# Attention over top-64 keys: a tile of a wide block and a tile of a narrow block share a step

## The reference

```python
x = x + 0.5 * ffn(layernorm(x));  x = x + attn(layernorm(x));  x = x + 0.5 * ffn(layernorm(x))

def attn(x, ...):                       # x: 4 x 1024 x 256, 16 heads of 64
    q, k, v = x @ Wq, x @ Wk, x @ Wv    # 4 memory keys and values stand ahead of k and v
    dots = einsum('bhid,bhjd->bhij', l2norm(q), l2norm(k)) * 10
    dots = einsum('hg,bgij->bhij', W_pre_th, dots)          # heads mixed
    dots = where(causal, mask_value, dots)
    vk = top_k(dots, 64)[0][..., -1:]                       # the 64th largest of a row
    attn = softmax(where(dots < vk, mask_value, dots))
    attn = einsum('hg,bgij->bhij', W_post_th, attn)         # heads mixed again
    out = einsum('bhij,bhjd->bhid', attn, v) * head_scale
    return (out * sigmoid(x @ Wg + bg)) @ Wo
```

## Time and profile before

| | |
|---|---|
| median of 3 runs | 3987.81 us (3987.8 to 4001.88) |
| the profiled execution | 3988.18 us, of which 3986.4 us span |
| PE busy | 3372.0 us, 85% of the span |
| DVE busy | 2934.9 us, 74% |
| ACT busy | 2528.9 us, 63% |
| POOL busy | 2038.6 us, 51% |
| DMA | 466.45 MB, 117 GB/s on average |
| attention, first to last operation | about 986 to 3709 us |

### The profile page before, as it was taken

How to read it: one execution, slowest core, us unless ns; L and a number is a source line. 1 busy time by engine, 2 the same in 40 slices (tenths; PEclk the granted TensorE clock), 3 DMA queues, 4 the chain that set the end, 5 groups by cost and what they waited for, 6 DMA issues and landing times. The chain is left out here.

```text
span 3986.4 us, 72866 instructions
## 1 busy us (share of the span) xinstructions
PE 3372.0 (85%) x22948; PEld 2142.8 (54%) x22948; DVE 2934.9 (74%) x6615; ACT 2528.9 (63%) x5825; POOL 2038.6 (51%) x5777
## 2 busy tenths in 40 slices
PE   4999999996788988888888857888988888988798
PEld 3444444442455655755555644555566555556566
DVE  3887777777478888667888876788886788887254
ACT  1343333333478789767888936788896788888231
POOL 0021222221577667577766737676675776667232
PEclk8999999999589999969999977899998899999899
DMA  2122222213455565245655314455543555651110
GB/s 105 69 95 84 80 84 86 79 75 115 124 148 164 165 170 134 71 126 159 169 169 167 97 40 129 144 170 169 166 107 82 143 156 167 171 137 51 52 33 27
DMA packets 362422, 466.45 MB, mean 117 GB/s; under 512 B 29524, under 2 KB 294100, under 8 KB 361560
## 3 DMA queue, kind: packets, MB, share of 16 engines
q1 hardware_dynamic: 361944, 461.02, 39.4%
HBM read 226.57 MB, written 234.36 MB: 116 GB/s over the span
## 5 line engine op out<-in xcount | busy, mean ns | idle before, releaser
L1005 ACT ACTIVATE junk<-D,nt 128x76 int8<-128x76 f32 (+62 forms) x1440 | 1070.6, 746 | 176.6 <-POOL nt L1090 138.5
L917 PE MATMUL banks<-kr,E 128*128 128x128 f32 (+1 forms) x4672 | 739.2, 309 | 190.5 <-issue 93.1
L917 PEld LDWEIGHTS banks<-kr,E 128*128 128x128 f32 (+1 forms) x4672 | 631.7, 211 | 302.9 <-issue 280.1
L890 PE MATMUL banks<-Sg,kpre 128*128 128x109 f32 (+51 forms) x1568 | 653.2, 517 | 17.7 <-DVE D L1211 8.7
L876 PE MATMUL banks<-kT,qT 64*128 64x343 f32 (+11 forms) x896 | 408.9, 540 | 182.3 <-DVE Sn L1200 161.1
L1028 ACT ACTIVATE AT<-banks 128x512 f32<-128x512 f32 (+3 forms) x768 | 346.0, 479 | 336.5 <-PE banks L937 169.5
L1290 DVE SCALAR_TENSOR_TENSOR E<-D,vk,E 128x12 f32<-128x12 f32 (+56 forms) x512 | 378.6, 757 | 211.0 <-DVE vk L1246 136.3
L1200 DVE COPY Sn<-banks 128x686 f32<-128x686 f32 (+7 forms) x448 | 376.9, 841 | 138.8 <-PE banks L877 127.1
L1226 DVE SCALAR_TENSOR_TENSOR W<-SG,sgn,W 128x76 f32<-128x76 int8 (+14 forms) x480 | 413.2, 900 | 83.7 <-POOL W L1106 81.7
L554 DVE RECIPROCAL a_ri<-a_rr 128x512 f32<-128x512 f32 x128 | 429.2, 3353 | 4.4
L937 PE MATMUL banks<-AT,V 128*64 128x64 f32 x9216 | 368.6, 232 | 56.4 <-issue 42.0
(11 more groups left out here) (188 smaller groups left out, 5547.0 us busy)
## 6 DMA issues: line engine op xcount, KB each, us to landing
score_scratch<-Sn SPq DMA_DIRECT2D x96, 343.0 KB, 3.2
q_scratch<-a_qn SPq DMA_DIRECT2D x32, 512.0 KB, 2.8
v_scratch<-a_vo SPq DMA_DIRECT2D x32, 512.0 KB, 3.7
k_scratch<-a_qn SPq DMA_DIRECT2D x32, 512.0 KB, 2.7
gate_scratch<-a_gs SPq DMA_DIRECT2D x32, 512.0 KB, 2.7
kT<-k_scratch SPq DMA_DIRECT2D x32, 512.0 KB, 4.8
qT<-q_scratch SPq DMA_DIRECT2D x32, 512.0 KB, 6.3
gateT<-gate_scratch SPq DMA_DIRECT2D x32, 512.0 KB, 11.8
```

The costliest lines, as they stand in the source:

```text
L890: out = nc.tensor.matmul(bank[:, 0:c], kpre[:].rearrange("p h r -> p (h r)"), Sg[:, g % 3, c0:c1], start=True, stop=not diagonal)
L917: out = nc.tensor.matmul(ps[5 + i % 2][0:rows, c % 4 * P:(c % 4 + 1) * P], E[:, g % 4, c * P:c * P + rows], kr[:, g % 4, :], start=True, s ...
L1005: nc.scalar.activation(out, D[:, e, 1:1 + n], ACT.Sign, bias=nt[:, r, e:e + 1], scale=-1.0, accum_out=cnt[:, r, e:e + 1]).then_inc(s[f"cnt ...
```

## The change

**Pairs.** A step no longer takes two tiles that follow each other. `place(g)` gives odd `g` a tile of a narrow block and even `g` a tile of a wide block: block 0 goes with block 7, 1 with 6, 2 with 5, 3 with 4. The wide lane runs 4 steps behind (`LAG`), so there are 260 steps, of which the first four have only a narrow tile and the last four only a wide one. Every other step has about 1040 keys in sum. The steps of batches follow each other without a boundary: the wide lane of pair 4-3 still runs while the narrow lane has begun with block 0 of the next batch.

**Buffers.** `Sg`, `SG`, `junk`, `W` and `E` are split into a wide and a narrow one, `D` has both side by side, `Sg` has two buffers for each lane (four in all), `qT` and `gateT` have two blocks. The wide tile is mixed into banks 2 and 3 (4 too for three pieces), the narrow tile into bank 4. `AT` holds both lanes, from either end.

**Order.** Count 3 and count 1 begin with the narrow tile, and `turned` stands behind count 3 in each step. `sides` and `closest` are two calls each, the wide tile's first, and stand in different slots. `SG` is free after `sides`, `W` after `closest`. `judge` has one operation less. `values` is cut in four quarters: one ahead of the unit in slot 1, one behind it, two at the start of the next step. `select` takes the narrow tile first.

**Units and loads.** Units of both blocks of a pair are made in 12 of 16 steps ahead of it, and a piece has at most 400 columns instead of 512 (in effect block 6 is cut in three pieces instead of two): 480 units instead of 448. The first pair's wide block is scored in the first two steps. Keys of a batch are loaded at once (all eight chunks), over four steps near the end of the batch before, as are values; the means of all blocks are worked out at once (`fore`) and copied when needed (`mean`).

```diff
 def pieces(n):
-    k = -(-n // 512)
+    k = -(-n // 400)
...
+LAG = 4
+NP = B * TURN
+S = NP + LAG
...
+def place(g):
+    w = g // 2 if g % 2 else g // 2 - LAG
+    if not 0 <= w < NP:
+        return None
+    i = w % TURN // TPB
+    return w // TURN, i if g % 2 else IB - 1 - i, w % TPB
...
+    def unit_steps(k):
+        q = (k - 2) // 16 + 1
+        j = (k - 2) % 16
+        slots = [range(0)] * 4
+        if k < 2:
+            n = UC[2] - UC[1]
+            return [range(UC[1] + n * (4 * k + i) // 8, UC[1] + n * (4 * k + i + 1) // 8) for i in range(4)]
...
             for k in range(S + 6):
-                held = (k - 5) % 4 == 0
-                if 0 <= k - 5 < S and not held:
-                    turned(2 * (k - 5))
-                if searched(k - 2):
-                    count(2 * (k - 2), 3)
-                    count(2 * (k - 2) + 1, 3)
...
+                count(k - 2, 3, True)
+                if 0 <= k - 5 < S:
+                    turned(2 * (k - 5))
...
+                count(k - 1, 1, True)
                 if 0 <= k - 5 < S:
                     turned(2 * (k - 5) + 1)
...
+            for i in range(UC[1] - 1):
+                scored([i])
+            for c in range(IB - 1):
+                fore(0, c)
+            scored([UC[1] - 1])
...
+                if k >= 12 and (k - 12) % 4 == 0 and (k - 12) // 4 < NV:
+                    values((k - 12) // 4, 0)
+                units(slots[1])
+                if k >= 12 and (k - 12) % 4 == 0 and (k - 12) // 4 < NV:
+                    values((k - 12) // 4, 1)
+                units(slots[2])
```

818 lines of the change are left out of this document (444 added, 374 removed).

## The result

The changed kernel takes **4154.9 us** (4 runs, 4151.6 to 4159.2) against 3989.3 us before: ratio 1.041 (95% interval 1.0385 to 1.0431), 166 us slower. I had forecast 3914 us, and the range to 4020 doesn't hold it. The profiled execution of the change spans 4157.4 us.

A forecast was written before the change was run, and what follows sets the result against it. DVE's work and flag stall (floor 8.86 us of a 10.3 us step) were taken as the bound, plus waits. Step 3 at 1105, 2482 for 259 steps and 26 for the search put the last exponentials at 3613: 3914 us, range 3825 to 4020.

The forecast's parts named there:

- The start: Run up to step 3: loads, key sums and 24 units of block 7 make it 93 us later than before.
- step 3 at about 1105: Sign for the run's beginning: first exponentials of step 3 at about 1105 us; at 1080 or 1130 it was mis-sized.
- The general search: Its one run, on a flagged row, now meets one wide and one narrow tile: 26 us instead of 40.6.
- at cost nothing: Keys and values loaded by batch over four steps are covered; if values aren't, some 3 us per step, 12 per batch.
- a load by batch holds up SP's queue: Sign named for being wrong: loading keys or values by batch stalls SP's DMA queue; no price given.
- The even step of 9.8 us: 233 uniform steps in the middle take 9.8 us each, 2283 us in all; ends 9.35 and 10.35.
- block 3 is the pattern: Uniform steps resemble block 3 of the kernel before: near the batch's mean load, 78.8 us per eight steps, 9.85 each.
- The end: Last steps, mostly without units: 16 at 8.3 us, four with only a wide tile at 6, two at 5.
- C: Rival, uneven products: TensorE's lumps of values and `post` cost as before; step 10.1, 3984 us, no change; chance 0.18.
- D: Rival, slower: POOL's small search operations, held up by DVE's long rows, lie on the path; step 10.3, 4031 us; chance 0.17.
- D's other sign: In the profile after, waits of PE for `AT` would show that POOL's small operations lie on the path.
- B: Rival, waits shrink: DVE's floor paces, DVE over 86% busy; step 9.35, 3809 us; chance 0.23.

The follow-up runs named there:

- e1: Changed kernel with each values load of 124 rows cut into one of 112 and one of 12 rows: 4044.4 us, ratio 1.0154.
- e2: Kernel before the change with the same cut of its values loads into 112 and 12 rows: 3932.8 us, ratio 0.9876.
- e7: e1 with each values event multiplying only its first chunk, the other chunks' products left out: 3923.7 us, ratio 0.9817.
- e12: e1 with VectorE's select over only the first half of each tile's columns: 3991.7 us, ratio 1.0013.
- e13: e1 with ScalarE's exponentials over only the first half of each tile's columns: 4039.3 us, ratio 1.0122.
- e9: e1 with even values events, five chunks for a wide block and four for a narrow one, same sum: 4039.2 us, ratio 1.0152.
- e4: e1 with ScalarE's count 3 of the wide tile moved behind that lane's `turned`: 4083.1 us, ratio 1.0248.
- e5: e1 with TensorE's `post` of the wide tile moved behind the next step's first mix: 4226.5 us, ratio 1.0595.
- e6: e1 with the second half of each values event behind the first mix, and gating behind the first take: 4063.8 us, ratio 1.0192.
- e11: e1 with the first slot of units behind both mixes and both takes: 4042.0 us, ratio 1.0168.
- e15: e1 with the first wide block's units on alternating banks (4014.0 us), plus unread TensorE products in steps without units or event: 4032.3 us, ratio 1.0125.

## Why the prediction was wrong

**The start: right as a sum.** 1121 forecast for step 5, 1121.7 measured in the change. The sign that I had named for it, step 3 at about 1105, did not come: step 3 begins at 1040.8, and 81 us for two steps stand behind it, since most of the 24 units lie behind step 3 and not ahead of it. The terms held one by one: the key sums take 11.6 us (12), the units 65 (67), and they end at 1094.4 where the sum had 1095.

**The general search: right.** The eight steps with it take 116.5 us where those of another batch take 89.2 (steps 83 to 90, 147 to 154): 27 us, forecast 26, before 40.6.

**The loads of values "at cost nothing": the step that failed first.** I had weighed bytes (2.4 MB per step, 245 GB/s) and priced the case that they aren't covered at "some 3 us per step, 12 per batch". Measured: two such loads per step cost 28 us per batch in their four steps against the cut version, 101 to 111 us in all. The price missed not the bytes but the spread: the loads kept under 4 packets in flight, two loads' packets took 12.5 to 14.6 us, longer than a step, and small loads behind them landed after 13 to 17 us. I had the load in view as a volume, and its form stood in the code, unchanged by the edit. Before, the same load stood alone in a block and cost 1.6 us, hidden among others; four steps with two each made it a queue. My last sentence, "I am wrong [...] if a load by batch holds up SP's queue", named a sign that came: two issues of these loads took 6.9 to 8.1 us together in each batch. I had given it no price of its own, and it is at most a part of the 28 us: the largest waits shown above are for loads and stores that landed late.

**The even step of 9.8 us: the step that failed second.** With the loads mended a step of batch 2 is 10.24 us: 233 steps by 0.44 are 103 us. The stretch itself agrees: steps 7 to 240 of e1 take 2413.6 us, where my sum has 2283 + 26 = 2309, 104 us more. The choice that failed was "block 3 is the pattern". It has VectorE's mean load (64.1 to 64.0 us), but TensorE's is 67.1 against a mean of 71.1, and ScalarE's 62.9 against 65.5. Between blocks 3 and 4, by TensorE's row, 71.1 us of work lie at 78.8 + 4.0/8.6 x 7.5 = 82.3 us, 10.3 a step. The same sum over e2's blocks, which have the loads mended as e1 has, gives 10.1 by TensorE's row (76.5 and 89.1 us at 65.2 and 78.9 us of TensorE, mean 70.2) and 9.8 by VectorE's; 10.24 was measured. These sums were made after the result. I had put TensorE aside by a rule of the Trainium skill (Perfetto Trace Analysis, "Identifying the Most-Contended Engine") that matmul busy time isn't a good measure of how close TensorE is to its roofline. By that row the sum comes within 0.1 us a step, and without it it missed by 0.44; so here the trace doesn't support the rule as I used it, to leave TensorE out of the comparison. (Its loads' row adds up to 388 us, 59% of the batch, and not 393; ScalarE in block 3 is busy 80%, not 81. Neither changes the sum.) What is shown is that TensorE's amount counts (e7, 121 to 134 us of 170), VectorE's in part (e12, 53 to 56 of 134), ScalarE's exponentials hardly (e13), and that neither the evening of large and small events (e9), nor four orders (e4, e5, e6, e11), nor added products at a higher granted clock (e15) brings anything. The steps with an event, which TensorE fills, are a part of it that the trace shows. That the end of the other steps is set now by one engine and now by another, and evening out the tiles doesn't change how often, fits all of this; it is argued and not shown by a run of its own.

**The end: 30 us short.** From step 240 to step 262 the sum has 133 + 24 + 10 = 167 us, and the change took 196.9: 151.4 for the 16 steps at 8.3, 45.5 for the last six, of which I had made 34. In e1 it is 192.5. No run looks into this stretch, so its cause stays open; it is what these steps take without units that was sized too low.

**The sum again**, by the marks of the two profiled executions (the change's took 4159.2 us): 3914 + 1 (start) + 110 (steps 7 to 240, the change against e1: the loads) + 104 (the same steps of e1 against the sum) + 30 (end) = 4159. Nothing of size is left over. Alone, the loads make it 4024 and the longer steps 4018, near the upper end of the range; together they leave it behind.

**The rivals.** C came out in size (10.1 a step in the stretches shown) and in part in cause: steps with an event are 2.7 us longer than the others, as they were before, but making the large and small ones alike brought nothing. D had the sign right, slower, and its mechanism fell. ScalarE's waits for `nt` (L1166, L1170, L1178) are 24.0 us in 48 steps, 0.50 a step, not above the 0.5 that I had named, and batch 1 before has 0.61. The operation that I had held up as the proof, L1089, got shorter, not longer, when every step has long rows. In batch 1 before, 180 of it take 64.05 us, 0.36 us each; the same operation, L1177, takes 32.74 us for 144 in the 48 steps, 0.23 each. One other operation did get longer, the first of each search: 0.19 us before (L1082), 0.64 after (L1170). In all, the operations of the search from its first to its last guess take 2.8 us a step before and after, where D had 0.5 to 1 us more. D's other sign did come: TensorE waits for `AT` 17.2 us in these 48 steps, 0.36 a step, where batch 1 before has 3.7 us in all; but turning `AT` earlier (e4) was slower, so that wait isn't the price either. B fell: VectorE is at 77% in those 48 steps. My mistake among the rivals was that each priced a uniform step. The case that only a few steps are hit, and each doubles, had no rival of its own.

## What to carry over

Ask of each DMA how many rows its slowest dimension has, and what that leaves of the 16 engines, before its bytes are weighed: cutting each load of 124 rows into 112 and 12 gave 51 us in a kernel where I had expected at most 0.3% and 101 to 111 us where two stood in a step. When a change makes uneven steps even, compare the mean of the old pieces, on every engine, with the piece that is taken as pattern; a gain is there only if the old time bends between them, and here it nearly lay on a line: the time of the eight blocks of the earlier trace rows is 1.12 to 1.20 times TensorE's busy time in each. Moving loads together changes their price, so a load that was hidden alone has to be priced again in company.

## What of the hardware was not expected

- A load of 124 rows of 4 KB kept 2.8 to 3.9 packets in flight; two such as 112 and 12 rows kept 9 to 12. Where two uncut ones stand in a step, an issue of such a load on SP took up to 5.1 us; in the kernel before at most 0.54. A load of 66 KB issued beside two of the former landed after 16.9 us; loads of 30 to 50 KB where no values were loaded took 3.4 to 5.8 us.
- Half of the columns in TensorE's 4672 products of `post` made the kernel 185 us slower: their median duration stayed at 275 ns (at full clock in both; 421 at 0.50 in both), and the granted clock of a batch fell from 0.92 to 0.80, with single steps wholly at 0.50.
- Adding TensorE work that nobody reads raised the granted clock (0.915 to 0.934, 0.919 to 0.943) and left the time as it was or 12 to 18 us longer.
